# A fused convolution-attention and mixture-of-experts kernel: the guards of the first and the last quad in two halves, two score banks lent for one stage less

## What is computed

```python
# 1. convolution attention, each image: q, k of 16 channels, v of 128; softmax over 1024 positions
x = x + softmax(q k^T) v
# 2. on the normalised tokens of each image
#    global attention, 8 heads of 16, over all 1024 tokens:
attn = softmax(q k^T / 4);  o = attn v
#    local attention, 4 heads of 32, over a window of 5 tokens; both fused by a 2-layer net;
#    layer norm, feed-forward, layer norm
t = t + block2(layer_norm(t))
# 3. 8 experts over all 8192 tokens, one expert a token by argmax, 1280 places an expert, in token order
t = t + experts(layer_norm(t))
```

## Time and profile before

| What | Value |
|---|---|
| Time, 3 runs | median 1701.35 us (1699.8 to 1703.33) |
| Profiled execution | span 1699.6 us, 24956 instructions; its time outside the span isn't recorded |
| TensorE | 1550.0 us busy (91%) |
| VectorE | 1310.6 us (77%) |
| ACT | 1004.8 us (59%) |
| GpSimd | 721.2 us (42%) |
| Chain that ended last | TensorE 63%, VectorE 18%, ACT 6%, transfers 5% |
| Mean granted TensorE clock | 0.952 of full speed |

### The profile page before, as it was taken

The page is one execution under the profiler, slowest core; times in us unless marked ns, Lnnn a source line. Parts: engine busy times, 40 slices in busy tenths (PEclk is TensorE's granted clock), DMA queues, the critical chain, the costliest instruction groups (busy, mean ns, idle before and its releaser), DMA issues.

```text
span 1699.6 us, 24956 instructions
## 1 busy us (share of the span) xinstructions
PE 1550.0 (91%) x8475; PEld 784.8 (46%) x8475; DVE 1310.6 (77%) x2791; ACT 1004.8 (59%) x1907; POOL 721.2 (42%) x1126
## 2 busy tenths in 40 slices
PE   6777999999999999999999999999989988879993
PEld 3523434543554345435543454435533432449992
DVE  4478898789888888897777878897869762647984
ACT  2302656667766776777666667666666576415543
POOL 4202411125642564246434444645465356224562
PEclk8866999999999999999999999999999997989997
DMA  2264650143224222422144212421163111033335
GB/s 73 83 162 150 225 148 19 35 137 110 81 82 128 85 82 82 135 77 82 47 126 121 81 57 91 125 92 55 60 165 100 66 39 46 7 89 108 108 118 214
DMA packets 122899, 165.38 MB, mean 97 GB/s; under 512 B 14134, under 2 KB 86891, under 8 KB 122772
## 3 DMA queue, kind: packets, MB, share of 16 engines
q1 hardware_dynamic: 115284, 153.60, 29.7%
q0 software_dynamic: 4608, 7.30, 1.3%
q10 hardware_dynamic: 2880, 2.88, 0.5%
HBM read 104.41 MB, written 61.15 MB: 97 GB/s over the span
## 4 chain that ended last, share of the span: by engine, by line
PE 63%; DVE 18%; ACT 6%; DMA 5%; issue 4%; POOL 3%; SPq 1%; POOLq 0%; ACTq 0%; DVEq 0%
PE bank L1624 11%; PE bank L1593 9%; PE bank L1612 9%; PE bank L1548 7%; DVE gmax L2257 6%; PE bank L1858 4%; PE bank L1465 4%; DVE cmax L2190 3%; PE bank L1540 2%; PE bank L1651 2%; PE bank L1661 2%; ACT prob L1984 2%; DMA kv_d<-lqkv 2%; PE bank L1567 1%; PE bank L1562 1%
## 5 line engine op out<-in xcount | busy, mean ns | idle before, releaser
L1984 ACT ACTIVATE prob<-bank 128x512 f32<-128x512 f32 x1024 | 572.3, 597 | 284.5 <-PE bank L1612 282.6
L2257 DVE TENSOR_REDUCE gmax<-bank 128x1 f32<-128x512 f32 x1024 | 657.4, 682 | 59.2 <-PE bank L1593 56.3
L1593 PE MATMUL bank<-k_stack,q_stack 96*128 96x512 bf16 x1024 | 398.6, 396 | 33.0 <-DVE gmax L2257 16.3
L1612 PE MATMUL bank<-q_stack,k_stack 99*128 99x512 bf16 x1024 | 393.9, 391 | 23.9 <-ACT prob L1984 16.9
L1624 PE MATMUL bank<-prob,v_tok 128*32 128x512 f32 x2048 | 279.6, 620 | 0.0
L1593 PEld LDWEIGHTS bank<-k_stack,q_stack 96*128 96x128 bf16 x1024 | 100.8, 99 | 259.8 <-DVE gmax L2257 145.0
L1372 POOL TENSOR_TENSOR lprod<-ls,kv_win 128x640 f32<-128x640 f32 x64 | 80.9, 1285 | 269.1 <-DVE ls L2316 269.1
L1612 PEld LDWEIGHTS bank<-q_stack,k_stack 99*128 99x128 bf16 x1024 | 100.0, 99 | 191.2 <-ACT prob L1984 117.0
L1365 POOL TENSOR_TENSOR lprod<-ql_tok,kv_win 128x640 f32<-128x640 f32 x64 | 99.6, 1576 | 137.9 <-DMA ql_tok<-ql_d 137.2
L1548 PEld LDWEIGHTS bank<-cv_tok,cprob 128*128 128x128 f32 x960 | 114.4, 192 | 22.3 <-DVE t_tok L2224 11.6
L1548 PE MATMUL bank<-cv_tok,cprob 128*128 128x129 f32 x960 | 121.1, 279 | 1.5 <-DVE t_tok L2224 0.5
(11 more groups left out here) (292 smaller groups left out, 2549.8 us busy)
## 6 DMA issues: line engine op xcount, KB each, us to landing
kv_win<-kv_d SPq DMA_DIRECT2D x32, 1280.0 KB, 5.5
kv_d<-lqkv SPq DMA_DIRECT2D x64, 128.0 KB, 2.6
gparts_d<-cprob SPq DMA_DIRECT2D x24, 256.0 KB
gparts_d<-parts SPq DMA_DIRECT2D x24, 256.0 KB
q_stack<-gparts_d SPq DMA_DIRECT2D x32, 192.0 KB, 3.1
k_stack<-gparts_d SPq DMA_DIRECT2D x16, 384.0 KB, 5.1
rows_d<-rows SPq DMA_DIRECT2D x10, 528.0 KB, 6.1
cprob<-rows_d SPq DMA_DIRECT2D x8, 660.0 KB, 5.6
```

Source lines behind the costliest of these rows:

```text
L1593: mm(max_ps[max_bank(n)][:, :], q_stack[quad][0:KROWS, h, i * P:(i + 1) * P], key_slot(b, quad)[0:KROWS, h, j * HN:(j + 1) * HN], start=Tr ...
L1612: mm(score_ps[n % 2][:, :], key_slot(b, quad)[0:KM, h, j * P:(j + 1) * P], q_stack[quad][0:KM, h, half * HN:(half + 1) * HN], start=True, ...
L1984: nc.scalar.activation(prob[:, g % 2, h, :], score_ps[n % 2][:, :], ACT.Exp).then_inc(exp_made, 1)
L2257: v.tensor_reduce(gmax[:, h, i, j:j + 1], max_ps[max_bank(n)][:, :], AX.X, ALU.max)\
```

## The change

The guards of the quads (batch 0, quad 0) and (batch 7, quad 1) are made in two halves of the queries; the other fourteen stay whole. In a split quad the first half's guard takes tiles 0 to 31; its transpose stands in the order of the max banks behind tile 33 (`GUARD_BEHIND = 2`), and its `guard_rows` are four transfers, one a head, in place of three. The second half's guard follows tile 63. Score tiles 0 to 31 wait for the first half, the others for the second. The step `guard` of the plan is divided into `guard_max` (VectorE) and `guard` (TensorE), and the max banks turn on from quad to quad by one common count (`MAX_TURN`), not from bank 0 anew.

The convolution of batch 1 gets banks 0, 4 and 5 up to its `conv_guard` only (that is for its maxima); its exponentials and products use bank 0 alone. In the plan, the scores of batch 0 now name `conv_guard` of batch 1 as something to wait for.

```diff
+SPLIT_GUARDS = [(0, 0), (B - 1, 1)]
+GUARD_BEHIND = 2
+def guards_of(b, quad):
+    return 2 if (b, quad) in SPLIT_GUARDS else 1
+def max_uses(b, quad):
+    tiles = [("max_tile", quad, n) for n in range(TILES)]
+    if guards_of(b, quad) == 1:
+        return tiles + [("guard", quad, 0)]
+    first = TILES // 2 + GUARD_BEHIND
+    return tiles[:first] + [("guard", quad, 0)] + tiles[first:] + [("guard", quad, 1)]
+MAX_USES = [(b, use) for b in range(B) for quad in range(QUADS) for use in max_uses(b, quad)]
+MAX_TURN = {u: n for n, u in enumerate(MAX_USES)}
...
-    "guard": [("dve", 1.15, 0.1), ("pe", 0.11, 0.3)],
+    "guard_max": [("dve", 1.15, 0.1)],
+    "guard": [("pe", 0.11, 0.3)],
...
 def maxima(s, a, quad):
+    guards = guards_of(a, quad)
+    for name, _, t in max_uses(a, quad):
+        if name == "guard":
+            s.add("maxima", a, ("guard", quad, t), (a, ("guard_max", quad, t)), banks=MAX_PS)
...
+        if (t + 1) % (TILES // guards) == 0:
+            s.add("maxima", a, ("guard_max", quad, t * guards // TILES), (a, ("max_tile", quad, t)))
...
-        s.add("scores", a, ("score_tile", quad, n), (a, ("guard_rows", quad)), (a, ("pv_group", quad, n // QH - 2)),
+        s.add("scores", a, ("score_tile", quad, n), (a, ("guard_rows", quad, n * guards_of(a, quad) // TILES)),
+              (a, ("pv_group", quad, n // QH - 2)), *([(1, ("conv_guard",))] if a == 0 else []),
               banks=SCORE_PS)
...
-    conv_half(s, 1, 0, EARLY_PS)
+    conv_half(s, 1, 0)
...
-        EARLY_USES = head_turns[1, ("conv_pv", HT - 1)] + 1
+        EARLY_USES = head_turns[1, ("conv_guard",)] + 1
...
+            def guard_rows(b, quad, k):
+                sp.wait_ge(max_free, max_turn(b, "guard", quad, k) + 1)
...
+                for h in range(QH):
+                    dst = q_stack[quad][KROWS:KM, h, t.start * P:t.stop * P].rearrange("s (t p) -> s t p", p=P)
+                    sp.dma_start(dst, gneg_rows[h * 3 * n:(h + 1) * 3 * n, :]).then_inc(landed, 16)
...
+            def max_fill(b, name, quad, n):
+                after(pe, max_free, max_turn(b, name, quad, n) - MAX_BANKS + 1)
+                return max_home(b, name, quad, n)
...
-                if n == 0:
-                    after(pe, guard_in[quad], (b + 1) * 48)
+                if n == 0 or n == TILES // 2 and guards_of(b, quad) == 2:
+                    guard_landed(pe, b, quad, n // (TILES // 2))
...
+            def guard_max(b, quad, k):
+                t = guard_tokens(b, quad, k)
...
+                dve.wait_ge(max_free, max_turn(b, "max_tile", quad, last) + 1)
...
+            def guard_rows(b, quad, k):
...
+                dve.wait_ge(max_full, max_turn(b, "guard", quad, k) + 1)
+                if k:
+                    guard_landed(dve, b, quad, 0)
...
+                v.tensor_copy(gneg_rows[0:n, :], max_home(b, "guard", quad, k)[:, :].bitcast(BF16)[0:n, 0:P])\
```

More of the change, by code:

```diff
@@ L115 @@
 TAIL_TURNS = len(TAIL_USES)
+SPLIT_GUARDS = [(0, 0), (B - 1, 1)]
[10 more added lines that the diff above has]
+MAX_TURN = {u: n for n, u in enumerate(MAX_USES)}
+GUARD_NO = {u: n for n, u in enumerate(u for u in MAX_USES if u[1][0] == "guard")}
 PARTS = {
@@ L462, in maxima @@
 def maxima(s, a, quad):
-    for t in range(TILES):
+    guards = guards_of(a, quad)
+    for name, _, t in max_uses(a, quad):
+        if name == "guard":
+            s.add("maxima", a, ("guard", quad, t), (a, ("guard_max", quad, t)), banks=MAX_PS)
+            s.add("maxima", a, ("guard_rows", quad, t), (a, ("guard", quad, t)),
+                  (a, ("guard_rows", quad, 0)) if t else (a, ("guard_rows", 0, guards_of(a, 0) - 1)) if quad
+                  else (a - 1, ("guard_rows", 1, guards_of(a - 1, 1) - 1)))
+            continue
         s.add("maxima", a, ("max_tile", quad, t), (a, ("key_stacks", quad)),
               (a, ("query_stacks", quad, t // (TILES // 2))), banks=MAX_PS)
-    s.add("maxima", a, ("guard", quad), (a, ("max_tile", quad, TILES - 1)), banks=MAX_PS)
-    s.add("maxima", a, ("guard_rows", quad), (a, ("guard", quad)),
-          (a, ("guard_rows", 0)) if quad else (a - 1, ("guard_rows", 1)))
+        if (t + 1) % (TILES // guards) == 0:
+            s.add("maxima", a, ("guard_max", quad, t * guards // TILES), (a, ("max_tile", quad, t)))
 def scores(s, a, quad):
@@ L994, in tail_count, with max_turn, max_home, guard_count @@
             return b * (TAIL_TURNS + 2) + 4 + TAIL_TURN[use]
-        def max_bank(n):
-            return n % MAX_BANKS
+        def max_turn(b, name, quad, n):
+            return MAX_TURN[b, (name, quad, n)]
+        def max_home(b, name, quad, n):
+            return max_ps[max_turn(b, name, quad, n) % MAX_BANKS]
+        def guard_count(b, quad):
+            return sum(16 * (QH if guards_of(n, quad) == 2 else 3) for n in range(b + 1))
+        def half_guard(b, quad, k):
+            return guards_of(b, quad) == 2 and k == 0
+        def guard_tokens(b, quad, k):
+            return slice(HT * k, HT * k + HT) if guards_of(b, quad) == 2 else slice(0, NT)
+        def guard_landed(eng, b, quad, k):
+            if half_guard(b, quad, k):
+                eng.wait_ge(half_guard_in, (SPLIT_GUARDS.index((b, quad)) + 1) * QH * 16)
+            else:
+                eng.wait_ge(guard_in[quad], guard_count(b, quad))
         def end_filled(eng, h, *use):
@@ L1575, in global_v @@
                 last.then_inc(tail_full, 1)
-            def max_fill(b, quad, n):
-                used = b * 2 * (TILES + 1) + quad * (TILES + 1)
-                if n >= MAX_BANKS:
-                    after(pe, max_free, used + n - MAX_BANKS + 1)
-                elif not (isinstance(b, int) and b == 0 and quad == 0):
-                    last = [k for k in range(TILES + 1) if max_bank(k) == max_bank(n)][-1]
-                    after(pe, max_free, used - TILES + last)
+            def max_fill(b, name, quad, n):
+                after(pe, max_free, max_turn(b, name, quad, n) - MAX_BANKS + 1)
+                return max_home(b, name, quad, n)
             def max_tile(b, quad, n):
-                max_fill(b, quad, n)
+                ps = max_fill(b, "max_tile", quad, n)
                 if n == 0:
@@ L2267, in guard_rows @@
-            def guard_rows(b, quad):
-                after(dve, max_full, (b * 2 + quad + 1) * (TILES + 1))
-                if quad == 0:
-                    after(dve, guard_in[1], b * 48)
-                else:
-                    after(dve, guard_in[0], (b + 1) * 48)
-                v.tensor_copy(gneg_rows[:, :], max_ps[max_bank(TILES)][:, :].bitcast(BF16)[0:3 * QH * NT, 0:P])\
+            def guard_max(b, quad, k):
+                t = guard_tokens(b, quad, k)
+                n = t.stop - t.start
+                last = ((k + 1) if guards_of(b, quad) == 2 else 2) * TILES // 2 - 1
+                dve.wait_ge(max_free, max_turn(b, "max_tile", quad, last) + 1)
+                wide = lambda m: m.rearrange("p (h t) -> p h t", h=QH)
+                parts_ = gneg_parts[:, :, :].rearrange("p s t -> p (s t)")[:, 0:3 * QH * n]\
+                    .rearrange("p (s h t) -> p s h t" if n == NT else "p (h s t) -> p s h t", s=3, h=QH)
+                neg_parts(gmax[:, :, t, :], wide(max_home(b, "guard", quad, k)[:, NEG_AT:NEG_AT + QH * n]), parts_,
+                          guard_step, GUARD_NO[b, ("guard", quad, k)] * NEG_STEPS)
```

58 lines of the change are left out of this document (32 added, 26 removed).

## The result

The changed kernel takes 1705.92 us (median of 10 runs, 1701.09 to 1710.79), the kernel before 1699.26 us beside it (median of 10, 1695.26 to 1703.33). The ratio of the timed runs is recorded as 1.0048, 95% interval 1.0033 to 1.0063: slower, where 1692.5 us was forecast. (The two medians by themselves give 1.0039; the text goes by the recorded ratios.) The profiled execution is the slowest of the ten, 1710.79 us, with a span of 1709.0 us, 9.4 us more than before.

A forecast was written before the change was run, and what follows sets the result against it. TensorE was taken to bound the long middle, with unused time at both ends. Against the 1699.6 us span, -7 + 1.2 - 1 - 4 + 2 = -8.8 gave 1690.8, or 1692.5 us by the runs' median; range 1679 to 1708.

The forecast's parts named there:

- One bank for the batch-1 convolution: Batch 1's convolution chain ends up to 6.8 us later, hidden by 10.8 us of slack at its key stacks: 0.
- First quad, scores earlier: Batch 0's first scores start near 136 instead of 170 us, filling unused TensorE time: -7 us, bounds -14.8 and 0.
- What the halves add: Extra VectorE guard steps and copy per split quad count in the first quad only; other additions hidden: +1.2 us.
- Bank turns: Max banks turning on through the quads give one tile more cover for the guard's copy: -1 us, bounds 0 and -4.4.
- Last quad: Thirty max tiles leave the full stretch for idle TensorE time behind 1390 us: -4 us, bounds -14.6 and +6.6.
- Order elsewhere: Other steps may change places in the planner's orders, 3.5 us either way: +2 us.
- head of batch 1 late: Rival: score work ahead of the one-bank convolution delays batch 1's key stacks beyond their slack: 1707 us, chance 0.20.
- signs of being wrong: Max tile waiting for k_stack near 230 us; score after 165; clock near 0.5 after 1390; middle idle up over 5 us.
- signs of being right: Score near 136–145 us; clock over 0.8; batch 1 max tile by 235; last-quad max tiles at 1390–1420, clock over 0.9.
- Low clock at the end: Rival: max tiles moved behind 1390 us run at the low clock, +6.6 in place of -4: 1703 us, chance 0.16.

The follow-up runs named there:

- e3: Kernel before with only the three max banks turning on through the quads, no guard halved, order of before: 1697.24 us, ratio 0.9984 to the kernel before.
- e9: Kernel before's order on every engine, no guard halved, the batch-1 convolution given one bank: 1707.89 us, ratio 1.0067 to the kernel before.
- e4: Changed kernel without halved guards: score banks lent for the head's maxima only, one bank for the batch-1 convolution, order planned anew: 1714.74 us, ratio 1.0094 to before.
- e1: Changed kernel with only the first quad's guard halved, loan included, one guard in the last quad: 1703.64 us, ratio 1.0020 to the kernel before.
- e8: Changed kernel with only the first guard halved, loan included, order of before from batch 1's first maxima on: 1705.92 us, ratio 1.0037 to the kernel before.
- e12: Changed kernel, only first guard halved, three banks kept for batch 1's first half convolution, scores behind it, planned anew: 1695.39 us, ratio 0.9985 to before.
- e2: Changed kernel with only the last quad's guard halved, first quad and loan as before: 1698.67 us, ratio 0.9995 to the kernel before.
- e16: Changed kernel with VectorE reading only 256 of 512 columns of batch 0's second-quad max tiles: ratio 1.0035 to the kernel before.
- e10: Changed kernel with only the first guard halved, two banks for the batch-1 convolution, order planned anew: 1710.98 us, ratio 1.0064 to the kernel before.
- e14: First guard halved, two banks for the batch-1 convolution, order of before behind batch 1's maxima: 1697.96 us, ratio 1.0012 to the kernel before.

## Why the prediction was wrong, step by step

Put one after the other, each step beside the last, the ratios give the whole: bank turns -0.16% (e3), one bank +0.83% (e9), its own order +0.27% (e4), the first half guard -0.74% (e1), the last one +0.28% (the changed kernel), together +0.48%. Only the second and the fourth have intervals that do not overlap. All but the last guard comes to +0.20%, 3.4 us, where -4.8 was forecast; the last guard comes to +0.28%, 4.8 us, where -4 was forecast.

**One bank for the batch-1 convolution: 0.** This step failed, in its size and in its cover. The chain's slip was sized at up to 6.8 us and measured 11.0 (42.1 against 31.1 us), 11.3 in the unchanged order. There the exponentials cost 5.3 us of it instead of 4.8 (on three banks the first eight come every 0.72 us on average, not 0.88), and the stretch with the four products 6.0 instead of 2.0: the price of a product was a wait of 0.49 us read from one of the second half, and the waits came to as much as 1.2. Worse was the cover. The 10.8 us of slack were read at the key stacks, and there they hold: 10.6 us late, 1.5 us felt. But bank 0 has a second customer behind the convolution, the head of batch 2, for which no row was read. The first channel transposes of batch 1 are copied at 188.7 us before, at 198.6 us after, and batch 2's maxima begin 55.5 and 56.7 us later: no slack at that place. In the order of before the slip stays (the head maxima of batch 7 in e9 are still 7.3 us late) and costs the 0.67% to 0.83%; in the changed kernel's own order it is down to 1.7 us at batch 6. ACT's timeline after, for the first of these numbers:

```profile
198.59 0.57 ACT L1950 ACTIVATE a_cm<-bank 128x512 f32<-128x512 f32 x1
```

**First quad, scores earlier: -7.** The place was right (138.21 us in the forecast 136 to 145; a clock of 1.00 from 145 to 175 us, forecast over 0.8), the worth was not a number of its own. TensorE's unused time counted as time won, as if TensorE set the end of that stretch. The same step measured -0.74% (12.6 us) beside one bank in its own order, -0.30% beside one bank in the order of before (e8 against e9, overlapping intervals), nothing with three banks (e12 against e3, each in its own order), +0.37%, +0.13% and +0.52% with two. That -7 lies among these is luck. In the fixed order the heads explain more of the time than TensorE's work does, as the table shows; why early scores cost time with two banks is open. The Trainium skill ("TensorE: Matmul & The Clock Gate", section "HAM oscillation — how this bites in real kernels") describes matmuls split by waits for transfers, whose clock falls back each time. Here the waits are for VectorE and ACT, and the trace agrees so far that the stretch from 135 to 175 us, with scores between the waits, went from 0.69 to 0.90. This clock did not shorten the kernel; and e3, in the order of before, has 0.79 there, so a part of the rise is spread.

**What the halves add: +1.2.** About right: the 16-column steps of the first quad take 0.17 to 0.18 us, the 32-column ones 0.19 to 0.23, and the four transfers 0.70 us each on the queue against 0.59. Around the halved guards no matmul or weight load waited more than 0.6 us for their rows.

**Bank turns: -1.** Within its bounds: the ratio of e3 gives -2.7 us, its interval reaches from -6 to +0.5. The max tiles' wait for the guard's copy, 4.4 us in 5 times before, is 2.8 us in one time in e3.

**Last quad: -4.** The premise failed. Thirty max tiles were to leave the full stretch; TensorE's row of max tiles after 1390 us in the changed kernel has eight, 8 x 0.22 = 1.8 us:

```profile
L1652 PE MATMUL bank<-k_stack,q_stack x8: 379/390/390, 1392.5 to 1398.4; 96*128 96x512 bf16 x8
```

Before, the last maximum ended at 1385.3 us, with the scores of the quad before still running: the tiles stood among those scores, and most stayed there, spread over a longer time (the quad's maxima start over 80.6 us, before 66.7, by the rows above). By itself the step is neutral (0.9995), with the first one it costs 0.28%, from two kernels whose intervals just overlap. The profiles put it at the end. The last attention exponentials before, in e1 and after:

```profile
L1984 ACT ACTIVATE prob<-bank x8: 592/594/597, 1454.8 to 1461.0; 128x512 f32<-128x512 f32 x8
```
```profile
L2046 ACT ACTIVATE prob<-bank x4: 591/594/597, 1457.1 to 1458.6; 128x512 f32<-128x512 f32 x4
```
```profile
L2046 ACT ACTIVATE prob<-bank x8: 588/594/606, 1456.1 to 1464.8; 128x512 f32<-128x512 f32 x8
```

From the start of the last of them to the end of the span it is 238.6 us before, 240.3 in e1 and 244.2 in the changed kernel. The other two kernels with this split and the hand-set shifts, e2 and e16, have 244.1 and 243.8; the fifteen without the split have 237.1 to 241.4. All three with the split were profiled in the slowest run of their kernel, so the size is uncertain. The guard's last copy comes at 1401.6 us, before at 1387.9, and the end's first products need the banks of the maxima; that this is the way was not tried, and neither was the clock there.

**Order elsewhere: +2, at most 3.5 either way.** Right in kind, too small in size: the order behind batch 1's maxima moved the time by 0.52% (e10 against e14), 9 us. For the loan alone, the new order is +0.27% (e4 against e9), not clear of noise.

**Of the rivals**, "head of batch 1 late" came, with part of its reason. It was put down to score work ahead of the convolution, and to a slip beyond the slack of the key stacks; one bank without any moved score makes a head late, and at a place without slack. That its price, 1707 us, is near the measured time is luck: it keeps -4 for the last quad, which measured +4.8. Of the signs of being wrong, TensorE's idle time in the middle was up by more than 5 us (7.4), and no max tile waited for the key stacks. Of the signs of being right, the first score and the clock came; the first max tile of batch 1 was at 237.1 us, not by 235, and the few max tiles behind 1390 us stood at a clock of 0.61. "Low clock at the end" is not separated: from 1390 to 1440 us the clock is 0.70 in the changed kernel, 0.79 in e2 with the same split, 0.73 before.

## What to carry to other kernels

Slack read at one consumer is the slack of that consumer; follow a shared bank to its next user before a longer stage is costed at nothing. Idle time of the busiest engine is not time won until a run shows it: here filling the same holes was worth anything from -0.74% to +0.52%, while two banks in place of one for a serial chain took the time from 1.0067 to 0.9975 in one fixed order. A late start in one place need not reach the end, so read the same step in later batches before the loss is put down to it. A fixed order tuned by hand makes every change of its input a change of its own size, so measure each part once in the old order.

## What the runs showed that was not expected

The same order begins its first maxima 3.6 us apart in two profiled executions (96.3 us in e3, 99.9 before), as much as most terms of the forecast; positions from single profiles are compared within a run, or by many of them. Two banks were enough to run 16 exponentials of 0.597 us in 28.5 us with their products between; three for the first half and one for the second took 31.1, one for both 42.4.
